# A decoder of two layers on one core: TensorE runs products that nobody reads ahead of the first steps of group 0 in three attentions

## The chip, the cores and the metric

One core of one Trainium2 chip runs the whole program. The metric is the device time of one execution in microseconds. The kernel before was timed in 3 runs, and one further execution was recorded by the profiler.

## The reference

The input x has 32 batches of 128 tokens of width 128, the context 32 x 128 x 96. Six blocks are added to x one after the other; each works on x normalised over its channels.

```python
x = x + self_attention(layernorm(x))              # layer 0, 16 heads of 8, rotary
x = x + cross_attention(layernorm(x), ctx)        # 16 heads of 8, scores clipped
x = x + gated_experts(layernorm(x))               # 8 experts, the best 2, and 2 shared
x = x + causal_attention(layernorm(x))            # layer 1, 16 heads of 8, rotary, causal
x = x + latent_attention(ctx, layernorm(x))       # 2 heads of 64, latents are the tokens of x
x = x + relu_experts(layernorm(x))                # 8 experts, the best 2, hidden size 512
```

An attention is softmax(q k^T / sqrt(d)) v, with projections for q, k, v and the output, and biases.

## The kernel before

The program is a row of phases, each a block in which the five engines have instruction streams of their own, with a barrier between. `load_setup` loads constants, x and weights. `attention` does self and cross attention in one phase and, in a later one, causal attention; `latent_attention` and `relu_experts` end the program. The 32 batches form 8 groups of 4 (`GB`), so that a group has 512 tokens (`GT`). Whatever concerns weights is done once a group, scores and softmax once a batch.

The order of the steps on each engine is written by hand in `ORDERS` (L195). For every batch n an engine goes through its list; a step such as `k^6` is done once a group, six batches ahead of the group's first batch, and a step without a number once a batch, ahead by what `AHEAD` says. In latent attention the number behind the name is always the lead. For self attention TensorE's list is

```python
"PE": "T s0 f0 m y f1 q^5 s1 k^6 x^7 w k2^6 q2^5 v^4",
```

so that group 0 begins with x, k, k2, q, q2 and v, one behind the other, before the first batch has any scores. The steps are these. `x` (L468) turns the normalised x into columns with 4 transposes into the bank PB; ScalarE rounds it (x_hi, L562) and VectorE makes the remainder (x_lo, L645). `k`, `k2`, `q`, `q2` (L482) project with three products of 512 columns into the same bank PB (L366 to L368), and each waits until VectorE (L613) or, in causal, ScalarE (L540) has read the projection before it. `v` projects with 12 products of 128 columns. POOL then adds the two halves of the rotation (L719), takes remainders (L728) and spreads keys and queries over the heads (L732). Per batch follow `s0` and `s1` (scores, L392, which VectorE reduces to maxima, L591), `m` (transpose of the maxima, L439), `T` (key scores, 12 products into the four banks T, L408 to L413), `f0` and `f1` (the maxima are subtracted, L425), the exponentials on ScalarE (L521), and `w` (weights times values, L452). In causal attention products with a constant (L377) start the scores with the mask.

Latent attention begins with `C` and `X` (L1658, transposes of context and x), then `P` (L1699, projection of a batch, five matrices in six products), `K` (L1709, transposes of q and k of a batch) and only then scores. TensorE starts once the setup and the mask rows (ScalarE, L1894) are there. `X` is followed on ScalarE by an affine step and a rounding, and on POOL by the remainder (L2178), for which `P` waits.

All of these products are fp32r except for the transposes and the weights times values. [...]

Of the kernel before, what the change touches and what calls it, by code (L numbers as in the profile page):

```python
# [19 lines left out]
P = 128  # L20
# [4 lines left out]
GT = GB * P  # L25
# [40 lines left out]
C_ID, C_ONES, C_MASK = 0, P, 5 * P  # L66
# [156 lines left out]
def attention(nc, phase, kinds, sb, bank, context=None, x_ready=None):  # L223
# [23 lines left out]
    cr = sb["const_r"]  # L247
# [13 lines left out]
    S, T = bank[:, 0:2 * GT], bank[:, 2 * GT:6 * GT]  # L261
# [13 lines left out]
    def steps(engine):  # L275


        for n in range(-10, NBT + 2):
            found = []
            for number, k in enumerate(kinds):  # L280
                order = ORDERS[k][engine].split()
                for place, step in enumerate(order):
                    name, _, lead = step.partition("^")
                    first = n + int(lead) if lead else n + AHEAD[name]
                    if first // B == number and not (lead and first % GB):
                        found.append((place / len(order), number, name, first // GB if lead else first))
            for _, _, name, i in sorted(found):
                yield name, i
# [9 lines left out]
    PIECES = ("k", "k2", "q", "q2", "v")  # L298
# [5 lines left out]
    with ExitStack() as ctx:  # L304
# [59 lines left out]
        def _(pe):  # L364
# [17 lines left out]
            def scores(n, pair):  # L382
                causal = kind(n) == "causal"
                if pair == 0:
                    pe.wait_ge(k_masked, n + 1)
                if 2 * n + pair > 0:
                    pe.wait_ge(max_done, 2 * n + pair)
                units = (2 * pair, 2 * pair + 1)
                if causal:
                    hide([S[:, u * GT:(u + 1) * GT] for u in range(2)], 0)  # L390
                for u in units:
                    mm = pe.matmul(s_bank(u), kq_hi[QUERY][(n // GB) % 2][rows_of(u), batch_cols(n)],  # L392
                                   k_hi_m[n % 2][rows_of(u), :, :], start=not causal, stop=True)
                mm.then_inc(scored, 1)

            def key_scores(n):
                causal, clip = kind(n) == "causal", kind(n) == "cross"
                pe.wait_ge(q_masked, 2 * n + 2)
                if n > 0:
                    pe.wait_ge(exp_done, 2 * n)  # L400
                g = (n // GB) % 2
                k_hi, k_lo, q_hi, q_lo = kq_hi[KEY][g], kq_lo[KEY][g], q_hi_m[n % 2], q_lo_m[n % 2]
                if causal:
                    for u in (0, 2):
                        hide([t_bank(u), t_bank(u + 1)], 1)
                out = [t_bank(u).rearrange("p (j q) -> p j q", j=U) for u in range(U)]
                for u in range(U):
                    pe.matmul(out[u], k_hi[rows_of(u), batch_cols(n)], q_hi[rows_of(u), :, :],  # L408
                              start=not causal, stop=False)
                for u in range(U):  # L410
                    pe.matmul(out[u], k_hi[rows_of(u), batch_cols(n)], q_lo[rows_of(u), :, :], start=False, stop=False)
                for u in range(U):
                    mm = pe.matmul(out[u], k_lo[rows_of(u), batch_cols(n)], q_hi[rows_of(u), :, :],  # L413
                                   start=False, stop=clip)
                    if clip and u % 2 == 1:
                        mm.then_inc(keyed, 1)

            def shift(n, pair):
                clip = kind(n) == "cross"
                if pair == 0:  # L420
                    pe.wait_ge(neg_max_done, n + 1)
                if clip:
                    pe.wait_ge(clipped, 2 * (n - B0) + pair + 1)
                for u in (2 * pair, 2 * pair + 1):
                    mm = pe.matmul(t_bank(u), cr[rows_of(u), C_ONES + u * P:C_ONES + (u + 1) * P],  # L425
                                   neg_max[n % 2][rows_of(u), :], start=False, stop=True, skip_group_check=clip)
                mm.then_inc(shifted, 1)

            def transpose_max(n):
                if kind(n) == "cross":  # L430
                    pe.wait_ge(max_clipped, n - B0 + 1)
                else:
                    pe.wait_ge(max_done, 2 * n + 2)
                if n > 0:
                    pe.wait_ge(neg_max_done, n)
                if n - 2 > 0:
                    pe.wait_ge(heads_done, n - 2)
                for j in range(U):
                    mm = pe.transpose(OM[:, j * P:(j + 1) * P], maxes[n % 2][:, j * P:(j + 1) * P], sb["ident"][:, :])  # L439
                mm.then_inc(max_transposed, 1)  # L440

            def weigh(n):
                pe.wait_ge(exp_done, 2 * n + 2)
                if n > 0:
                    pe.wait_ge(heads_done, n)
                pe.wait_ge(neg_max_done, min(n + 3, NBT))
                pe.wait_ge(pb_read, pb_uses["v", n // GB])
                for of, c in ((lambda u, j: V[(n // GB) % 2][:, n % GB, U * u + j, :], 0),
                              (lambda u, j: head_ones[:, j, :], P)):
                    for j in range(U):  # L450
                        for u in range(U):
                            mm = pe.matmul(OM[rows_of(u), c:c + P], of(u, j), probs[n % 2][:, u, j, :],  # L452
                                           start=j == 0, stop=j == U - 1)
                mm.then_inc(weighted, 1)
# [6 lines left out]
            def out_project(n):  # L461
                pe.wait_ge(heads_done, n + 1)
                bank_free("y", n)
                c = ATT[kind(n)] * P
                pe.matmul(PB[:, 0:P], o_t[n % 2][:, :], sb["w_out"][:, c:c + P], start=True, stop=True)\
                    .then_inc(out_projected, 1)
# [15 lines left out]
            def project(name, G):  # L482
# [9 lines left out]
                    mm = split_matmul(PB, w, (hi[:, :], lo[:, :]))  # L492
                mm.then_inc(projected, 1)

            for step, i in steps("PE"):
                if step == "T":
                    key_scores(i)
                elif step in ("f0", "f1"):
                    shift(i, int(step[1]))
                elif step == "y":  # L500
                    out_project(i)
                elif step in ("s0", "s1"):
                    scores(i, int(step[1]))
                elif step == "m":
                    transpose_max(i)
                elif step == "w":
                    weigh(i)
                elif step == "x":
                    transpose_x(i)
                elif step == "c":  # L510
                    transpose_c(i)
                else:
                    project(step, i)
# [950 lines left out]
def latent_attention(nc, phase, sb, ps, t, ready, routed):  # L1464
# [3 lines left out]
    X = sb["x"]  # L1468
    TR, PL, PC, KT, S, T, O, M = ps
    cr, cols = sb["const_r"], sb["cols"]  # L1470
    ident, ident_r = sb["ident"][:, :], cr[:, C_ID:C_ID + P]
# [21 lines left out]
    def steps(engine):  # L1493

        for n in range(-14, B + 24):
            for step in ORDERS["latent"][engine].split():
                name = step[:min(step.find(c) for c in "+-^" if c in step)]
                once = step[len(name)] == "^"  # L1500
                batch = n + int(step[len(name) + once:])
                if not 0 <= batch < B:
                    continue
                if not once:
                    yield name, batch
                elif name in ("L", "R", "R1", "EX", "GG", "PL"):
                    if batch in LAST:
                        yield name, LAST[batch]
                elif batch % GB == 0:
                    yield name, batch // GB  # L1510
# [12 lines left out]
    with ExitStack() as ctx:  # L1523
# [49 lines left out]
        at_or_after, start = buf("at_or_after", [P, N_TILES, E1]), buf("start", [P, N_TILES])  # L1573
# [78 lines left out]
        def _(pe):  # L1652
# [120 lines left out]
            pe.wait_ge(setup_steps, SETUP)  # L1773
            pe.wait_ge(masks_made, 1)
            pe.wait_ge(filled, FILLED)
            for step, i in steps("PE"):
                if step in ("X", "C"):
                    transpose_inputs(step, i)
                else:
                    {"P": project, "K": transpose_keys, "s": scores, "T": key_scores, "m": transpose_max, "f": shift,  # L1780
                     "w": weigh, "o": transpose_heads, "y": out_project, "Z": transpose_rows, "L": make_logits,
                     "R": count_earlier}[step](i)
# [641 lines left out]
```

## Time and profile before

| | us |
|---|---|
| median of 3 runs | 1434.62 |
| lowest and highest | 1428.91, 1439.69 |
| the profiled execution's own time | 1435.96 |
| its span in the profile | 1434.2 |
| TensorE, VectorE, ScalarE, POOL busy | 84%, 61%, 47%, 54% |
| phases: self and cross from | 20 |
| causal from | 700 |
| latent from | 967 |

The span is what the records of the execution cover, 1.8 us less than its own time. The profile names instructions by their line in the kernel, the tile written and the tile read; PE is TensorE, DVE VectorE, ACT ScalarE. Where a row gives idle time, the name behind it is what the engine waited for. [...]

### The profile page before, as it was taken

What the parts mean: (1) busy time and instruction counts of PE and PEld (TensorE: products, weight loads), DVE (VectorE), ACT (ScalarE), POOL (GpSimd) and SP (SyncE); (2) the same over time, 40 slices, a digit from 0 to 9 for tenths busy, and PEclk for the clock granted to TensorE, in tenths of its full rate; (3) what the DMA queues carried; (4) which work ended last, traced back from release to release, by engine and by line L of the source; (5) the groups of instructions that cost most, each with busy time, mean ns of one, the idle gap of its engine ahead of it and who ended that gap; (6) DMA issues with size and microseconds to landing.
All of it is one profiled execution on the core that took longest, in us unless ns stands there. A gap on an engine that the chain in (4) does not pass through costs nothing. (4 is left out here: it accounts for less than half of the span.)

```text
span 1434.2 us, 33962 instructions
## 1 busy us (share of the span) xinstructions
PE 1197.7 (84%) x12478; PEld 901.5 (63%) x12478; DVE 878.1 (61%) x2007; ACT 674.8 (47%) x1298; POOL 768.1 (54%) x870
## 2 busy tenths in 40 slices
PE   1899998788888874999799999984999993199992
PEld 0577775555555563666467777764899983088881
DVE  3688876599999955666255666555888843122223
ACT  1345444344545422455345545437888631055551
POOL 3777873555666511444455555525776757344452
PEclk9999998799999985999789999996999955599996
DMA  9910000000000000000000000000000001256656
GB/s 346 380 56 10 2 2 15 14 15 15 14 15 7 2 2 1 1 1 0 1 2 2 2 2 3 2 2 23 12 13 2 20 25 52 78 192 201 196 192 179
DMA packets 58863, 75.27 MB, mean 52 GB/s; under 512 B 13246, under 2 KB 40003, under 8 KB 58576
## 3 DMA queue, kind: packets, MB, share of 16 engines
q1 hardware_dynamic: 53328, 63.59, 13.8%
q0 software_dynamic: 4544, 8.47, 1.7%
q8 instruction: 101, 1.65, 0.5%
q10 hardware_dynamic: 832, 1.09, 0.2%
q14 instruction: 58, 0.48, 0.1%
HBM read 40.24 MB, written 31.70 MB: 50 GB/s over the span
## 5 line engine op out<-in xcount | busy, mean ns | idle before, releaser
L591 DVE TENSOR_REDUCE maxes<-bank 128x8 f32<-128x1024 f32 x192 | 234.4, 1221 | 56.6 <-PE bank L392 55.1
L521 ACT ACTIVATE self_probs<-bank 128x1024 f32<-128x1024 f32 x128 | 129.1, 1022 | 46.1 <-PE bank L425 45.7
L1429 POOL DMA_INDIRECT returned<-relu_y,relu_slots x78 | 76.7, 984 | 93.8 <-DVE relu_y L1404 81.3
L1372 ACT ACTIVATE relu_hidden<-bank,cols 128x256 f32<-128x256 f32 x156 | 74.0, 474 | 94.0 <-PE bank L1330 80.5
L528 ACT ACTIVATE self_neg_max<-bank 128x512 fp32r<-128x512 f32 x64 | 38.2, 597 | 149.9 <-PE bank L439 149.9
L732 POOL TENSOR_TENSOR self_k_hi_m<-self_kq_hi,const 128x512 fp32r<-128x512 f32 x64 | 66.6, 1041 | 78.4 <-ACT self_kq_hi L549 78.4
L1330 PE MATMUL bank<-relu_s,relu_w_tile 128*128 128x256 f32 x312 | 94.3, 385 | 0.5 <-DVE relu_s L1398 0.5
L1338 PE MATMUL bank<-relu_hidden,relu_w_tile 128*128 128x256 f32 x312 | 92.5, 379 | 0.0
L1398 DVE COPY relu_s<-bank 128x256 f32<-128x256 f32 x39 | 16.6, 425 | 110.5 <-issue 81.1
L597 DVE TENSOR_SCALAR bank<-bank 128x1024 f32<-128x1024 f32 x64 | 78.2, 1223 | 3.3 <-PE bank L413 3.3
L601 DVE RECIPROCAL self_recip<-bank 128x128 f32<-128x128 f32 x64 | 61.2, 957 | 30.2 <-PE bank L452 28.2
L2215 POOL DMA_INDIRECT routed<-latent_rows,latent_place_i x64 | 63.0, 984 | 30.8 <-issue 16.6
L732 POOL TENSOR_TENSOR causal_q_lo_m<-causal_kq_lo,const 128x512 fp32r<-128x512 f32 x32 | 33.3, 1041 | 84.5 <-PE bank L425 84.4
L452 PE MATMUL bank<-self_probs,values 128*32 128x128 f32 x2048 | 73.1, 286 | 1.4 <-ACT self_neg_max L528 1.2
L452 PE MATMUL bank<-self_probs,head_ones 128*32 128x128 f32 x2048 | 70.8, 280 | 0.0
L425 PE MATMUL bank<-self_neg_max,const_r 32*128 32x512 f32 x256 | 62.0, 475 | 9.7 <-DVE bank L597 6.3
L521 ACT ACTIVATE causal_probs<-bank 128x1024 f32<-128x1024 f32 x64 | 64.5, 1022 | 5.2 <-PE bank L425 2.7
L732 POOL TENSOR_TENSOR self_q_lo_m<-self_kq_lo,const 128x512 fp32r<-128x512 f32 x64 | 66.7, 1042 | 0.3 <-PE bank L425 0.2
L732 POOL TENSOR_TENSOR self_q_hi_m<-self_kq_hi,const 128x512 fp32r<-128x512 f32 x64 | 66.6, 1041 | 0.0
L452 PEld LDWEIGHTS bank<-self_probs,values 128*32 128x32 f32 x2048 | 54.9, 113 | 18.6 <-issue 15.9
L439 PE MATMUL bank<-ident,maxes 128*128 128x128 f32 x384 | 65.2, 294 | 0.5 <-POOL maxes L755 0.3
L1338 PEld LDWEIGHTS bank<-relu_hidden,relu_w_tile 128*128 128x128 f32 x312 | 59.3, 190 | 8.3 <-ACT relu_hidden L1372 0.2
(380 smaller groups left out, 3434.9 us busy)
## 6 DMA issues: line engine op xcount, KB each, us to landing
relu_w_tile<-in_w_ffn SPq DMA_DIRECT2D x39, 512.0 KB
routed<-blank SPq DMA_DIRECT2D x1, 19760.0 KB, 60.9
relu_slots<-routed SPq DMA_DIRECT2D x39, 130.0 KB
relu_back<-returned SPq DMA_DIRECT2D x16, 256.0 KB, 4.4
x_all<-in_x SPq DMA_DIRECT2D x8, 256.0 KB, 8.2
x_before<-x_all SPq DMA_DIRECT2D x8, 256.0 KB, 2.7
out_x<-x_all SPq DMA_DIRECT2D x8, 256.0 KB, 4.0
self_ctx_in<-in_ctx SPq DMA_DIRECT2D x8, 192.0 KB, 2.6
```

Of the source, the lines that this page charges most:

```text
L425: mm = pe.matmul(t_bank(u), cr[rows_of(u), C_ONES + u * P:C_ONES + (u + 1) * P], neg_max[n % 2][rows_of(u), :], start=False, stop=True, sk ...
L439: mm = pe.transpose(OM[:, j * P:(j + 1) * P], maxes[n % 2][:, j * P:(j + 1) * P], sb["ident"][:, :])
L452: mm = pe.matmul(OM[rows_of(u), c:c + P], of(u, j), probs[n % 2][:, u, j, :], start=j == 0, stop=j == U - 1)
L521: act.activation(probs[n % 2][:, 2 * pair:2 * pair + 2, :, :].rearrange("p u j q -> p (u j q)"), T[:, 2 * pair * GT:(2 * pair + 2) * GT], ...
L591: dve.tensor_reduce(out.rearrange("p j u -> p u j"), S.rearrange("p (u j k) -> p u j k", u=2, j=U), AX.X, ALU.max, negate=True).then_inc(m ...
L597: dve.tensor_scalar(t, t, CLAMP / scale, -CLAMP / scale, ALU.min, ALU.max).then_inc(clipped, 1)
L732: pool.tensor_tensor(out[n % 2][:, :, :], src[(n // GB) % 2][:, batch_cols(n)].bitcast(F32).unsqueeze(1).broadcast_to([P, U, P]), slots.un ...
L1330: pe.matmul(HT[i % 2][:, 0:TT], w_tile[t % NW][:, c * P:(c + 1) * P], s[t % 2][:, :], start=True, stop=True)\
L1338: pe.matmul(YT[t % 2][:, 0:TT], w_tile[t % NW][:, F1 + c * P:F1 + (c + 1) * P], hidden[i % C1][:, :], start=c == 0, stop=c == C1 - 1).then ...
L1372: act.activation(hidden[i % C1][:, :], HT[i % 2][:, 0:TT], ACT.Relu, bias=sb["cols"][:, bass.ds(r + (COL_RELU + c), 1)]).then_inc(hidden_d ...
L1429: pool.indirect_dma_start(returned[:, :], bass.IndirectOffsetOnAxis(ap=slots[t % NX][:, b, P:P + 1].bitcast(I32), axis=0), y[t % NY][:, b, ...
L2215: pool.indirect_dma_start(routed[:, :], bass.IndirectOffsetOnAxis(ap=place_i[u % 3][:, k, b:b + 1], axis=0), rows[G % 4][:, k, n % GB, :], ...
```

## The change

In both functions TensorE gets a helper `idle_passes` of 8 products of 512 columns. Their operands are constants (the identity and the block of ones), they write to T, which no step has in use yet, and nothing reads what they write. They wait for nothing. They are issued ahead of the steps x, k, k2, q, q2 and v of group 0 in self attention (6 times), x, k, q and v of group 0 in causal attention (4 times), and C, X of group 0 and P, K of batch 0 in latent attention (4 times). Cross attention's groups are numbered from 8 on, so that it has none. The helper stands in front of the step's own waits. Nothing is removed and no other engine's stream is changed.

```diff
@@ attention
+            def idle_passes():
+
+                for _ in range(8):
+                    pe.matmul(T[:, 0:GT], cr[:, C_ID:C_ID + P], cr[:, C_ONES:C_ONES + GT], start=True, stop=True)
+
             for step, i in steps("PE"):
+                if step in ("x",) + PIECES and i == 0:
+                    idle_passes()
@@ latent_attention
+            def idle_passes():
+
+                for _ in range(8):
+                    pe.matmul(T[:, :], ident_r, cr[:, C_ONES:C_ONES + GT], start=True, stop=True)
+
             for step, i in steps("PE"):
+                if step in ("X", "C", "P", "K") and i == 0:
+                    idle_passes()
```

`PIECES` is ("k", "k2", "q", "q2", "v").

TensorE's stream at the start of self attention, before (L472 is x, each trio L366 to L368 a projection):

```order
L363 UNCONDITIONAL_BRANCH
L472 MATMUL bank<-ident,self_xn 128x128 x4
L366 MATMUL bank<-self_x_hi,w_hi 128x512
L367 MATMUL bank<-self_x_lo,w_hi 128x512
L368 MATMUL bank<-self_x_hi,w_lo 128x512
L366 MATMUL bank<-self_x_hi,w_hi 128x512
L367 MATMUL bank<-self_x_lo,w_hi 128x512
L368 MATMUL bank<-self_x_hi,w_lo 128x512
L366 MATMUL bank<-self_x_hi,w_hi 128x512
```

and with the change, where L498 is the product of `idle_passes`:

```order
L363 UNCONDITIONAL_BRANCH
L498 MATMUL bank<-const_r 128x512 x8
L472 MATMUL bank<-ident,self_xn 128x128 x4
L498 MATMUL bank<-const_r 128x512 x8
L366 MATMUL bank<-self_x_hi,w_hi 128x512
L367 MATMUL bank<-self_x_lo,w_hi 128x512
L368 MATMUL bank<-self_x_hi,w_lo 128x512
L498 MATMUL bank<-const_r 128x512 x8
L366 MATMUL bank<-self_x_hi,w_hi 128x512
L367 MATMUL bank<-self_x_lo,w_hi 128x512
L368 MATMUL bank<-self_x_hi,w_lo 128x512
L498 MATMUL bank<-const_r 128x512 x8
```

Eight products have come ahead of the transposes and ahead of each projection; the order of the rest is the same. TensorE's stream at the start of latent attention, before (L1666 is C or X, L1654 to L1656 P):

```order
L1666 MATMUL bank<-ident,latent_cn 96x128 x4
L1666 MATMUL bank<-ident,latent_xn 128x128 x4
L1666 MATMUL bank<-ident,latent_cn 96x128 x4
L1654 MATMUL bank<-latent_w_hi,latent_x_hi 128x384
L1655 MATMUL bank<-latent_w_lo,latent_x_hi 128x384
L1656 MATMUL bank<-latent_w_hi,latent_x_lo 128x384
L1654 MATMUL bank<-latent_w_hi,latent_c_hi 128x256
L1655 MATMUL bank<-latent_w_lo,latent_c_hi 128x256
L1656 MATMUL bank<-latent_w_hi,latent_c_lo 128x256
```

and with the change, where the lines of this function are 7 numbers further on and L1786 is the product of `idle_passes`:

```order
L1786 MATMUL bank<-const_r 128x512 x8
L1673 MATMUL bank<-ident,latent_cn 96x128 x4
L1786 MATMUL bank<-const_r 128x512 x8
L1673 MATMUL bank<-ident,latent_xn 128x128 x4
L1673 MATMUL bank<-ident,latent_cn 96x128 x4
L1786 MATMUL bank<-const_r 128x512 x8
L1661 MATMUL bank<-latent_w_hi,latent_x_hi 128x384
L1662 MATMUL bank<-latent_w_lo,latent_x_hi 128x384
L1663 MATMUL bank<-latent_w_hi,latent_x_lo 128x384
L1661 MATMUL bank<-latent_w_hi,latent_c_hi 128x256
L1662 MATMUL bank<-latent_w_lo,latent_c_hi 128x256
```

The second group stands between C and X of group 0, the third between the C of group 1 and the first P; the fourth comes after three P, ahead of K.

## Rows read from the trace of the kernel before

**Rows 1.** The page: busy time of the engines (1), TensorE's clock in 40 slices (2).
```profile
PE 1197.7 (84%) x12478; PEld 901.5 (63%) x12478; DVE 878.1 (61%) x2007; ACT 674.8 (47%) x1298; POOL 768.1 (54%) x870
...
PEclk9999998799999985999789999996999955599996
```

**Rows 2.** Timeline of TensorE, self: start, us, instruction, count [idle before, releaser].
```profile
25.57 1.11 PE L472 MATMUL bank<-ident,self_xn 128*128 128x128 f32 x4 [25.57 <-ACT self_xn L556]
28.09 0.79 PE L366 MATMUL bank<-self_x_hi,w_hi 128*128 128x512 f32 x1 [1.41 <-DVE self_x_lo L645]
28.68 0.63 PE L367 MATMUL bank<-self_x_lo,w_hi 128*128 128x512 f32 x1
29.11 0.63 PE L368 MATMUL bank<-self_x_hi,w_lo 128*128 128x512 f32 x1
...
38.05 0.48 PE L366 MATMUL bank<-w_hi,self_x_hi 128*128 128x128 f32 x1 [0.84 <-DVE self_by_sin L613]
...
40.46 0.41 PE L368 MATMUL bank<-w_hi,self_x_lo 128*128 128x128 f32 x1
...
48.79 0.80 PE L366 MATMUL bank<-self_x_hi,w_hi 128*128 128x512 f32 x1 [0.84 <-DVE self_by_cos L613]
...
55.91 0.80 PE L408 MATMUL bank<-self_q_hi_m,self_kq_hi 32*128 32x512 f32 x4
...
57.36 0.48 PE L392 MATMUL bank<-self_k_hi_m,self_kq_hi 32*128 32x512 f32 x2
...
61.28 0.51 PE L408 MATMUL bank<-self_q_hi_m,self_kq_hi 32*128 32x512 f32 x4
```

**Rows 3.** Timeline of VectorE: the first instruction behind the barrier, self and causal.
```profile
20.25 0.87 DVE L637 BATCH_NORM_STATS2 self_stats<-x_all 128x6 f32<-128x128 f32 x4 [0.30 <-PEq L110]
...
700.45 0.87 DVE L637 BATCH_NORM_STATS2 causal_stats<-x_all 128x6 f32<-128x128 f32 x4 [0.32 <-PEq L889]
```

**Rows 4.** Windows around causal's start: from:to, length, busy of each engine, PEclk.
```profile
702.00:704.00 2.00, 0.00 (x0) 0.00 (x0) 0.00 (x0) 0.02 (x1) 1.68 (x4) 0.67 0.00 0
...
726.00:728.00 2.00, 1.74 (x9) 0.77 (x5) 1.11 (x1) 0.91 (x3) 1.00 (x1) 0.86 0.00 0
```

**Rows 5.** Timeline of TensorE, last product before causal and causal's start.
```profile
698.74 0.66 PE L1021 MATMUL bank<-ident,ffn_y 128*128 128x128 f32 x4 [0.69 <-ACT ffn_y L1051]
705.68 1.11 PE L472 MATMUL bank<-ident,causal_xn 128*128 128x128 f32 x4 [6.29 <-ACT causal_xn L556]
708.21 0.79 PE L366 MATMUL bank<-causal_x_hi,w_hi 128*128 128x512 f32 x1 [1.41 <-DVE causal_x_lo L645]
...
715.81 0.80 PE L377 MATMUL bank<-const_r 64*128 64x256 f32 x4
...
727.11 0.40 PE L367 MATMUL bank<-causal_x_lo,w_hi 128*128 128x512 f32 x1
727.35 0.39 PE L368 MATMUL bank<-causal_x_hi,w_lo 128*128 128x512 f32 x1
```

**Rows 6.** Timeline of TensorE and of ScalarE, latent's start.
```profile
978.64 1.09 PE L1666 MATMUL bank<-ident,latent_xn 128*128 128x128 f32 x4 [1.15 <-ACT latent_cf L1833]
984.68 1.09 PE L1666 MATMUL bank<-ident,latent_cn 128*96 128x128 f32 x4 [4.96 <-ACT latent_cn L1857]
985.55 0.69 PE L1654 MATMUL bank<-latent_w_hi,latent_x_hi 128*128 128x384 f32 x1
...
994.48 0.90 PE L1714 MATMUL bank<-ident,latent_unit 128*128 128x128 f32 x3 [2.27 <-DVE latent_unit L1947]
...
968.27 3.71 ACT L1894 ACTIVATE latent_mask_rows<-mask_by_row,latent_masked 128x4096 fp32r<-128x4096 uint8 x1 [7.25 <-POOL latent_one L2225]
```

**Rows 7.** A window of latent's start, in columns as in rows 4.
```profile
988.00:990.00 2.00, 1.82 (x8) 1.33 (x6) 0.77 (x6) 2.00 (x6) 1.14 (x4) 0.65 0.00 0
```

**Rows 8.** Timeline of POOL: a sum in self, the low part of x in latent.
```profile
38.07 1.28 POOL L719 TENSOR_TENSOR self_full<-self_by_cos,self_by_sin 128x512 f32<-128x512 f32 x1 [3.70 <-DVE self_by_sin L613]
...
984.23 1.27 POOL L2178 TENSOR_TENSOR latent_x_lo<-latent_xf,latent_x_hi 128x512 fp32r<-128x512 f32 x1
```

## Prediction

> **What bounds the kernel now.** I read the page first: TensorE is busy for 84% of the span and every other engine much less [rows 1]. The reader should see that an added TensorE instruction costs nothing only where the engine waits. The row PEclk says where TensorE's clock is high; it also shows the sag at the seventh and eighth slice, where self attention hands over to cross. Next come the three places of the change, in TensorE's order of time.
>
> Self attention, first steps [rows 2]. The record of the clock can't be trusted here: it says 0.9 or more from the start. But two products of 512 columns start 0.43 us apart (28.68 and 29.11), which is 1.2 GHz, and twelve of them take 1.45 us (55.91 to 57.36). The first four of the same twelve take 0.80 us there and 0.51 us at 61.28. So the clock rose near 57.4 us, after the engine had been almost without a gap since 48.79. Until then it ran at half speed for 32 us. In these 32 us the projections k, k2, q, q2 start 2.49 us apart, (38.05 - 28.09)/4. The engine idles 0.84 us in each of these steps but the first, waiting for VectorE to empty the one bank. VectorE's first instruction at 20.25 [rows 3] dates the barrier, so TensorE sits free from about 20.3 to 25.57.
>
> Causal attention [rows 4, 5]. The last product before it starts at 698.74 and ends near 699.4. The granted clock is at the 2.4 level until about 702.7 (0.67 as the mean of 702 to 704) and 1.2 GHz until about 726.5 (0.86 in 726 to 728). Here, at the high level, two products of 512 columns are 0.24 us apart (727.11, 727.35). Latent attention [rows 6, 7]: TensorE waits for the mask rows until 972.0 and begins C about 976.4 (X at 978.64, less 1.15 us idle and C's 1.1). It is at 1.2 GHz until about 989.4 (0.65 in 988 to 990), having been busy since 984.68.
>
> **The price of a group.** The change adds 14 groups of 8 products of 512 columns and removes nothing. A group is 8 x 0.43 = 3.4 us at 1.2 GHz and 8 x 0.24 = 1.9 us at 2.4 GHz. None of them waits for a semaphore, so each starts the moment the products before it are done. What is queued behind is the step itself, and after it everything in TensorE's order. Only idle time in front of a step hides a group.
>
> [...]
>
> **Self attention.** Group 1, before x, runs from 20.3 to 23.7 and is hidden. The four transposes begin at 25.57 as before and are off the array by 26.4. Group 2, before k, costs 3.4 us at 1.2 GHz and ends at 29.8, where k could start at 28.09: +1.7 us. From 25.57 on TensorE is never idle. When does the clock rise? Nearest rows: it rose 4.7 us after the engine became busy in latent (984.68 to 989.4) and 8.6 us after in self (48.79 to 57.4). Both ends are kept: 30.3 or 34.2 us. I take the earlier, since the gaps are gone altogether. A step is then 3 products and a group, 11 x 0.24 = 2.7 us, against 2.49 before. The release by VectorE needs 2.49 - 3 x (0.43 - 0.24) = 1.9 us and hides inside. With +0.4 for k's first product, v starts 1.7 + 0.4 + 4 x 0.2 = 2.9 us late. It has 12 products of 128 columns, which take 2.6 us at 1.2 GHz (38.05 to 40.46 and one more); it saves half, 1.3, so it ends 1.6 us late. For POOL's chain, which starts with the sum at 38.07 [rows 8], the delay is about 1.9 us. With the late rise all this is 2 us worse, since one step takes 11 x 0.43 = 4.7 us.
>
> From v to the key scores of batch 1 at 61.28 everything runs at 2.4 GHz instead of 1.2. It saves only where TensorE is the link: four projections of group 1 at 3 x 0.19 = 0.6 each (2.4), the twelve key score products, which go four at a time, 0.6, four pairs of scores at 0.3 (1.2), a transpose of maxima and the shifts 0.7, which go by the same ratio. That is 4.9 us; VectorE's reductions and POOL's masks, which lie between, do not get faster. Net 1.6 to 1.9 - 4.9 = -3 us, or -1 us with the late rise. I take -3. The bounds are -5 (no group lengthens anything) and +10.5 (the clock stays low through all groups: 1.7 + 4 x (4.7 - 2.49)).
>
> **Causal attention.** The barrier falls at about 700.3 [rows 3]. Group 1 then runs at 2.4 GHz to 702.2 and is hidden, since the transposes wait until 705.68. In before, the clock fell 3.3 us after the last product. Now 3.4 us of idleness (702.2 to 705.68) lie before the transposes, so it may or may not hold. If it falls, group 2 costs 3.4 us from 706.4 and k starts at 709.8 instead of 708.21: +1.6. The clock rises by 710.4, q and v follow 2.7 instead of 2.43 us apart (+0.5), and v saves 1.3: the first scores, 715.81 before, come 0.8 late. From there to 726.5 the scores with their mask products, k, q and a transpose save about 3 us on the chain; net -2.2. If the clock holds, group 2 ends at 708.3, nothing is late, and the net is -3.9. I take -2.8; the bounds are -3.9 and +6.1 (1.6 + 2 x 2.25, clock low throughout).
>
> **Latent attention.** Group 1 starts at 972.0 [rows 6] and ends at 975.4, hidden. Group 2, before X, sits between 977.2 and 980.6 at 1.2 GHz: X, at 978.64 before, comes 2 us late. Its consumer on POOL, the low part of x, stood behind other POOL work until 984.23 [rows 8], so this too is hidden. Then TensorE idles until 984.68, so it is at 1.2 GHz. Group 3 stands directly before P(0), which had no gap in front of it (985.55): +3.4 us, of which the higher clock gives back 0.6 in P(0) and P(1). ScalarE and the norms follow late; POOL's inverse had 1 us of slack, so K(0), at 994.48 before, is some 1.8 us late. Group 4 before it, 1.9 us, shares the 2.27 us gap that the profile shows there. Behind K(0) the clock is high instead of low, which gives back about 1 us (by the same halving of three more projections) before the engine is full again. Net +1; bounds -1 (all groups in gaps) and +4.5 (clock low: 3.4 + 1.1).
>
> **Sum.** -3 - 2.8 + 1 = -4.8 us. All three kinds of attention are followed by a long stretch in which TensorE is nearly full, so a shift at the start should carry to the end. Made against the profiled execution's own 1435.96 us it gives 1431.2; the median of the runs is 1.3 us lower, 1434.62, and would give 1429.8. I say 1430.5.
>
> [...]
>
> **The rivals.**
> 1. The groups lengthen the path by more than the clock returns. One mechanism, in self attention: the single bank PB passes between TensorE and VectorE, and each of k2, q, q2, v now has 3.4 us of passes in front of it where only 0.84 us was idle. Each step at 1.2 GHz costs 4.7 - 2.49 = 2.2 us. The gain of 4.9 is eaten when the delay at v exceeds it, that is when the clock rises later than about 37 us. For it: the record of the clock says nothing reliable there, and once it took 8.6 us. Against it: in latent and causal it rose sooner, with gaps between. If the clock never rose within the groups: +10.5 + 6.1 + 4.5 = +21, 1457 us. With the rise a step or two late in each place: +2 to +6, about 1439.
> 2. The clock rises within or right after group 1 and holds over the short gaps: -5 - 3.9 - 1 = -10, about 1425. For it: group 1 is 3.4 us without a gap. Against it: in before the clock fell 3.3 us after the last product ahead of causal, and in latent 3.4 us of idleness remain ahead of 984.68.
> 3. The start gets shorter but POOL or VectorE, not TensorE, sets when batch 1 begins, or the clock's sag at the handover to cross (slices 7 and 8) falls otherwise and takes the gain or doubles it: about 0, 1435.
>
> **How the numbers follow.** Forecast (-2 to -8): 0.50. Rival 1: 0.15, of which 0.02 for the full 21 us. Rival 2: 0.15. Rival 3: 0.20. The forecast's own terms reach from 1427 to 1434; the runs of before spread over 11 us by themselves. The range takes in rival 2, rival 3 and the mild part of rival 1, and a median's own spread beyond them: 1421 to 1441. This measurement tells a difference from no change at about 1%, 14 us; faster by more would need every bound at its best and luck besides (0.04), slower by more needs the clock to stay low (0.03), and the rest, 0.93, lies within 1%.
>
> **What would show it.** In the changed profile: the 8 passes before x lie ahead of 25.6 us; spacing drops from 0.43 to 0.24 us between 29 and 34 us; v's first product starts near 41 us; the key scores of batch 1 start near 58 instead of 61.3; in causal the first scores start near 716.6 less the shift, and in latent P(0) is about 3 us further behind its C(1) than now. I am wrong if products are still 0.43 us apart after v, if v starts later than 43 us, or if the key scores of batch 1 start no earlier than before.

## The result, and the profile after

The changed kernel took 1440.03 us in the median of 20 runs (1434.59 to 1448.00), the kernel before 1435.95 us in 20 runs (1428.91 to 1445.33). The ratio is 1.0034, with a 95% interval from 1.0020 to 1.0048: slower by 0.34%, 4.9 us. I had forecast 1430.5 us, 4 to 5 us faster.

The profiled execution of the changed kernel took 1448.00 us, the longest of the 20. So the two traces are 12 us apart where the medians are 4 us apart, and the traces can't simply be subtracted. The page of the changed kernel, in the form of [rows 1]:

```profile
PE 1233.3 (85%) x12590; PEld 929.0 (64%) x12590; DVE 876.0 (61%) x2007; ACT 674.0 (47%) x1298; POOL 767.0 (53%) x870
...
PEclk9699998899999985899969999997999975599996
```

TensorE is 36 us busier. In the row PEclk three slices are lower than before: the second (36 to 72 us, 6 instead of 9), the 17th (578 to 615 us, in the experts, 8 instead of 9), and the 21st (723 to 759 us), where 6 stands and before had 7 and 8 in the 20th and 21st. The second and the 21st lie right behind the steps that the change touches.

PEclk is the granted clock of TensorE as a share of full speed. Low means 0.50 from here on and high 1.00. In the changed kernel's trace products of 512 columns start 0.427 us apart at 0.50 (26.07 to 29.06 us) and 0.227 us apart at 1.00 (35.22 to 38.88). These are the levels that the prediction calls 1.2 and 2.4 GHz.

TensorE's timeline at the start of self attention, in the columns of [rows 2]; L498 is the product of the added groups:

```profile
19.78 3.38 PE L498 MATMUL bank<-const_r 128*128 128x512 f32 x8 [19.78 <-PEq L110]
25.10 0.65 PE L472 MATMUL bank<-ident,self_xn 128*128 128x128 f32 x4 [1.93 <-ACT self_xn L563]
25.51 3.33 PE L498 MATMUL bank<-const_r 128*128 128x512 f32 x8
...
29.70 2.00 PE L498 MATMUL bank<-const_r 128*128 128x512 f32 x8
...
39.10 0.22 PE L366 MATMUL bank<-w_hi,self_x_hi 128*128 128x128 f32 x1
...
41.62 0.63 PE L472 MATMUL bank<-ident,self_xn 128*128 128x128 f32 x4 [1.07 <-DVE values L630]
43.12 0.79 PE L392 MATMUL bank<-self_k_hi_m,self_kq_hi 32*128 32x512 f32 x2 [0.87 <-POOL self_k_hi_m L739]
45.23 0.79 PE L392 MATMUL bank<-self_k_hi_m,self_kq_hi 32*128 32x512 f32 x2 [1.33 <-DVE maxes L598]
...
55.57 0.80 PE L408 MATMUL bank<-self_q_hi_m,self_kq_hi 32*128 32x512 f32 x4
...
62.94 0.80 PE L408 MATMUL bank<-self_q_hi_m,self_kq_hi 32*128 32x512 f32 x4
```

Up to v nearly all came as forecast. Group 1 is hidden, group 2 takes 3.3 us, the next ones 2.0 us, and v's first product starts at 39.10. What follows is the surprise: the four transposes at 41.62 still take 0.63 us, but the scores at 43.12 take 0.79, and at 55.57 and 62.94 the first of the twelve key score products take 0.80 us. That is the size at the low clock of [rows 2]. The key scores of batch 1 start at 62.94 instead of 61.28. The clock itself, in windows of this stretch (from:to, length, busy time of PE, PEld, DVE, ACT, POOL, then PEclk, DMA share and GB/s):

```profile
26.00:28.00 2.00, 2.00 (x6) 1.55 (x6) 1.47 (x5) 0.38 (x1) 0.40 (x1) 0.50 1.06 382
28.00:30.00 2.00, 2.00 (x7) 1.55 (x7) 0.48 (x5) 0.00 (x0) 1.21 (x3) 0.64 1.06 383
...
42.00:44.00 2.00, 1.04 (x5) 0.29 (x3) 0.74 (x2) 0.60 (x1) 2.00 (x3) 0.77 1.06 383
44.00:46.00 2.00, 0.77 (x3) 0.33 (x3) 1.96 (x5) 0.00 (x0) 2.00 (x3) 0.50 1.05 381
...
68.00:70.00 2.00, 2.00 (x32) 1.57 (x34) 1.56 (x2) 1.83 (x4) 1.37 (x2) 0.50 1.06 381
70.00:72.00 2.00, 2.00 (x56) 1.70 (x50) 0.55 (x2) 0.23 (x1) 2.00 (x3) 0.90 1.06 380
```

It rose at 29.4 us, near the 30.3 forecast. It had been high once before, toward the end of group 1: that group took 3.38 us and the transposes behind it 0.65, where e1 below, low throughout, shows 3.75 and 1.12. Behind the idle 1.93 us ahead of the transposes it fell at 26.0, so that group 2 ran at the low clock (0.50 in 26 to 28). It fell again at 43.1, behind v, where the engine works only 1.04 of 2 us, and then stayed at 0.50 until 70.4, 27 us, through windows in which TensorE was full or nearly so. In before it was high from 57.4 to 241.9. Causal attention has the same, in the columns of [rows 5] and [rows 4]:

```profile
715.10 0.77 PE L472 MATMUL bank<-ident,causal_xn 128*128 128x128 f32 x4 [3.15 <-ACT causal_xn L563]
715.52 3.65 PE L498 MATMUL bank<-const_r 128*128 128x512 f32 x8
719.02 0.39 PE L366 MATMUL bank<-causal_x_hi,w_hi 128*128 128x512 f32 x1
...
725.48 0.50 PE L377 MATMUL bank<-const_r 64*128 64x256 f32 x4
...
727.74 0.50 PE L377 MATMUL bank<-const_r 64*128 64x256 f32 x4 [1.33 <-DVE maxes L598]
...
730.09 0.80 PE L377 MATMUL bank<-const_r 64*128 64x256 f32 x4 [0.83 <-DVE maxes L598]
...
752.82 0.60 PE L425 MATMUL bank<-causal_neg_max,const_r 32*128 32x512 f32 x2
```

```profile
728.00:730.00 2.00, 1.25 (x10) 0.64 (x8) 1.29 (x2) 0.60 (x1) 2.00 (x3) 0.79 0.00 0
730.00:732.00 2.00, 1.92 (x7) 1.28 (x8) 0.96 (x2) 0.00 (x0) 2.00 (x3) 0.50 0.00 0
...
750.00:752.00 2.00, 2.00 (x17) 1.08 (x14) 0.36 (x1) 0.00 (x0) 0.00 (x0) 0.50 0.00 0
752.00:754.00 2.00, 2.00 (x12) 1.29 (x13) 0.00 (x0) 1.08 (x2) 0.00 (x0) 0.74 0.00 0
```

The first scores (725.48) come 14.6 us behind the phase's first VectorE aggregate, at 710.89; before it was 14.35 (715.81 and 701.46). So the groups cost the path 0.2 us here, although the clock fell at 715.5, behind 3.15 us of idleness, and group 2 took 3.65 us; it was back at 718.9. But the clock falls again at 729.2, in the gaps of 1.33 and 0.83 us around the scores, and is back only at 753.1. Those are 24 us at the low clock, and TensorE is busy in all but the first microsecond of them. In before the clock fell as well and was low for just as long, from 702.7 to 726.6; but the first 13 us of that were idle time and sparse projections.

Latent attention, in the columns of [rows 6]; L1786 is the added product:

```profile
999.95 1.09 PE L1673 MATMUL bank<-ident,latent_cn 128*96 128x128 f32 x4 [5.21 <-ACT latent_cn L1871]
1000.69 3.76 PE L1786 MATMUL bank<-const_r 128*128 128x512 f32 x8
1004.25 0.52 PE L1661 MATMUL bank<-latent_w_hi,latent_x_hi 128*128 128x384 f32 x1
...
1011.06 2.67 PE L1786 MATMUL bank<-const_r 128*128 128x512 f32 x8
1013.56 0.49 PE L1721 MATMUL bank<-ident,latent_unit 128*128 128x128 f32 x3
```

Here a group took 3.8 us in front of P(0) at the low clock (998.8 to 1005.6), where 3.4 was forecast, and 2.7 us in front of K(0), where 1.9 was.

To see what was the change and what was chance I cut all traces into stages. Each entry is the distance between the starts of two VectorE instructions: phase start of self (time 0) to the first output of self (o_t of batch 0), and so on. The causal stage runs from its first aggregate of moments to the third o_t, the latent stage from its first aggregate to the fifth heads, all in us:

| kernel | self, start | self to cross, o_t 30 to 40 | experts, groups 0 to 3 | causal, start | latent, start |
|---|---|---|---|---|---|
| before | 67.83 | 87.59 | 36.36 | 55.57 | 58.57 |
| the change | 72.48 | 86.86 | 43.03 | 61.54 | 61.20 |
| the change, again (e8) | 64.09 | 87.80 | 36.34 | 61.53 | 59.89 |
| self groups (e1) | 65.86 | 90.12 | 36.44 | 55.60 | 58.64 |
| causal groups (e2) | 67.87 | 87.79 | 42.85 | 57.14 | 57.72 |
| causal groups, again (e7) | 68.08 | 91.60 | 36.38 | 61.54 | 58.62 |
| latent groups (e3) | 67.98 | 88.96 | 43.08 | 55.55 | 59.44 |
| hidden groups (e4) | 66.35 | 91.54 | 36.37 | 55.40 | 58.41 |
| causal bridged (e5) | 68.05 | 87.78 | 36.34 | 54.79 | 59.58 |
| all bridged (e6) | 64.08 | 91.22 | 43.03 | 53.32 | 58.98 |
| self and causal bridged (e9) | 62.14 | 87.97 | 36.40 | 53.30 | 58.25 |
| self bridged (e10) | 63.83 | 91.18 | 36.30 | 55.56 | 58.73 |
| bridges alone (e11) | 67.96 | 88.02 | 36.39 | 54.77 | 59.61 |

The columns of the handover to cross and of the experts jump by 4 and 6.7 us between kernels that are equal there. The 6.7 us of the experts are in the first trace of the changed kernel and in e2, e3 and e6; in each of them the clock came back only at 585 to 589 us instead of 564 to 575. They have nothing to do with the change: in e3 nothing is changed ahead of the experts, and the change's second trace (e8) does not have them. The rest of the program, behind the fifth heads of latent, is no steadier: it took 405.4 us in before, 399.5 and 407.1 in the two traces of the change, and 397.8 to 412.2 in all. So the time of a single trace says little here. The stretch behind causal's start is steady: from the third o_t to the first aggregate of the latent phase all 13 traces take 213.1 us. What causal's start loses or wins is there in full at the end of that phase.

### The profile page after: what moved, and what is told of

It reads as the page before. It is cut to its first block and busy times, and to the rows that moved or that the text cites. A ratio compares the mean times of both kernels' runs of the same rounds, so it can differ in the third digit from the quotient of the medians.

```text
span 1446.2 us, 34185 instructions
## 1 busy us (share of the span) xinstructions
PE 1233.3 (85%) x12590; PEld 929.0 (64%) x12590; DVE 876.0 (61%) x2007; ACT 674.0 (47%) x1298; POOL 767.0 (53%) x870
## 5 line engine op out<-in xcount | busy, mean ns | idle before, releaser
L1249 POOL TENSOR_TENSOR ffn_hidden<-ffn_product,ffn_gate 128x512 f32<-128x512 f32 x32 | 40.9, 1281 | 46.9 <-ACT ffn_gate L1058 40.0
## 6 DMA issues: line engine op xcount, KB each, us to landing
routed<-blank SPq DMA_DIRECT2D x1, 19760.0 KB, 61.5
```

## The experiments

In all of them the ratio is that of 5 rounds against the kernel before on the same chip, with its 95% interval. Absolute times of different batches are not compared, since the kernel before itself took 1437.35, 1443.36 and 1434.75 us in the three batches.

**The parts one by one.** Self alone (e1):

```diff
-                if step in ("x",) + PIECES and i == 0:
+                if kinds[0] == "self" and step in ("x",) + PIECES and i == 0:
                     idle_passes()
@@ latent_attention
-                if step in ("X", "C", "P", "K") and i == 0:
-                    idle_passes()
```

> Only the 6 groups of self attention. Theory F (the clock is won too early: it rises near 30 us, falls again near 43 us in the gaps behind v, and comes back only near 70 us instead of 57): +2 to +5 us against before, low clock in most of 44 to 65 us, key scores of batch 1 (61.28 us before) at 62 or later. Rival O (only the groups' own time on TensorE costs, the clock is neutral): k, k2, q, q2 are 2.5 us apart as before, v ends no later, so 0 to +1 us. Rival N (the loss is luck in stretches that the change does not touch): 0.

Measured: 1.0002 (0.9976 to 1.0028). The trace is 2.0 us ahead at the first output; the clock rose near 29 us (group 2 still took 3.4 us, k's first product behind it 0.39), fell at 46.1 and was back at 52.9. So the low spell can be as short as 6.8 us. With the two traces of the change there are now three draws of this stage, that is three outcomes between which chance decides: 72.48, 64.09 and 65.86, mean 67.5, against 67.8 to 68.1 in the six traces that have no groups in self (before, e2, e3, e5, e7 and e11). Three traces that spread over 8 us fix no mean, but the runs of e1 agree with it: no difference, within 4 us. The expectation of theory F, +2 to +5 us and the key scores of batch 1 at 62 or later, was wrong for self; they started at 59.30.

Causal alone (e2), the same with `kinds[0] == "causal"`:

> Only the 4 groups of causal attention. Theory F: the clock falls within some 5 us behind v and stays low for over 15 us while TensorE is full: the second output of causal attention +3 to +6 us later, counted from the phase's first instruction. Rival O: at most +1 us. Rival N: 0.

Measured: 1.0066 (1.0042 to 1.0089), on 6 runs only. The trace has a low spell from 727.1 to 740.7, 14 us of full work, and the stage is 1.6 us longer. The interval excludes O and N; but the trace shows less than the ratio, so it was run again (e7):

> The causal groups alone once more, for the interval and a second trace. Theory F: again +3 to +10 us, with the clock down for 10 to 24 us behind v. If it comes out within 2 us of before, the first result was chance.

Measured: 1.0050 (1.0025 to 1.0075) on 12 runs, 7 us. The windows of its trace:

```profile
722.00:724.00 2.00, 1.52 (x10) 0.90 (x10) 0.97 (x2) 0.06 (x1) 2.00 (x3) 0.95 0.00 0
724.00:726.00 2.00, 1.27 (x6) 0.82 (x6) 1.26 (x2) 0.54 (x1) 2.00 (x3) 0.50 0.00 0
...
744.00:746.00 2.00, 2.00 (x20) 1.45 (x18) 1.01 (x1) 0.00 (x0) 0.00 (x0) 0.50 0.00 0
746.00:748.00 2.00, 2.00 (x16) 1.01 (x8) 0.00 (x0) 0.43 (x1) 0.00 (x0) 0.57 0.00 0
748.00:750.00 2.00, 2.00 (x44) 1.50 (x46) 1.03 (x1) 1.93 (x3) 0.75 (x1) 1.00 0.00 0
```

The clock fell at 723.8 and rose at 747.7, again 24 us, and the stage is 6.0 us longer than in before. Most of what is left to the changed kernel is this.

Latent alone (e3), with the first condition taken out and the second left in:

> Only the 4 groups of latent attention. Here the groups before P and K stand on the path: Rival O gives +2 to +3 us in this phase, Theory F adds nothing to that (in the trace with the change the clock was high from 1012 us on). Rival N: 0.

Measured: 1.0011 (0.9993 to 1.0029). The stage is 0.9 us longer than in before, and 1.3 and 2.6 in the two traces of the change. The ratio can't tell +1.6 us from nothing. Nor do the traces settle it: the eight without groups in latent reach from 57.72 to 59.61 (mean 58.7), the four with all of them from 58.98 to 61.20 (mean 59.9). About +1.2 us is likely, not shown.

Only the groups in idle time (e4):

```diff
-                if step in ("x",) + PIECES and i == 0:
+                if step == "x" and i == 0:
                     idle_passes()
-                if step in ("X", "C", "P", "K") and i == 0:
+                if step == "C" and i == 0:
                     idle_passes()
```

> Only the three groups that stand in idle time (before x in self and causal, before C in latent). Rival O: 0, since nothing on the path gets longer. Theory F: 0 as well, within 1 us, since the clock has no reason to be higher behind v than before; the first projections may start at the high level. If it is 2 us or more slower, the groups do harm by what they do to the clock later, not by their place.

Measured: 0.9988 (0.9964 to 1.0012), no difference. The causal stage is 55.40 us, as in before, and the first output of self is 1.5 us ahead. In causal the clock fell at 712.0 and was back at 732.4.

**The change once more** (e8, no edit):

> [...] Theory F: +3 to +6 us against before; in causal a fall of the clock within 6 us behind v. The places before causal (between cross attention and the experts) may come out anywhere within 8 us of the first trace.

Measured: 1.0045 (1.0020 to 1.0070). In causal the clock falls at 716.6 and rises at 740.5, 24 us again, and the stage is 61.53 us to the first trace's 61.54. In self it is 3.7 us faster than before: there it was high from behind group 1 on (the transposes at 25.29 take 0.66 us, group 2 2.11), fell at 44.2, and came back at 51.0. So the first trace's loss in self was a draw, the loss in causal was not.

**Bridging the gaps behind v.** If the falls are what cost, products in those gaps should turn the loss into a gain. In causal (e5):

```diff
-            def idle_passes():
+            def idle_passes(count=8):
 
-                for _ in range(8):
+                for _ in range(count):
...
+            BRIDGE = {("s1", 0): 6, ("x", 1): 2, ("s0", 1): 4}
...
+                if kinds[0] == "causal" and (step, i) in BRIDGE:
+                    idle_passes(BRIDGE[step, i])
```

with the groups of causal attention kept and those of self and latent left out.

> The 4 groups of causal attention and, in the gaps behind v, 6 products before the second scores of batch 0, 2 before x of group 1 and 4 before the first scores of batch 1. Theory F: the clock does not fall behind v, and the loss turns into a gain: 4 to 8 us faster than the run with the causal groups alone, against before -3 to +1 us; the second output of causal 2 to 4 us earlier within the phase than before. Rival O: another 0 to 2 us slower than the causal groups alone, since TensorE has more to do. If the clock falls all the same, the gaps are not what sends it down.

Measured: 1.0016 (0.9995 to 1.0037), against 1.0050 for e7 in the same batch. By the ratios that is 5 us less, and the stage went from 61.54 to 54.79 us, 0.8 below before. The windows:

```profile
718.00:720.00 2.00, 2.00 (x12) 1.17 (x10) 0.94 (x1) 0.00 (x0) 1.92 (x3) 1.00 0.00 0
...
730.00:732.00 2.00, 2.00 (x17) 1.41 (x16) 1.09 (x4) 1.97 (x3) 1.46 (x3) 1.00 0.00 0
...
734.00:736.00 2.00, 2.00 (x20) 1.36 (x18) 0.88 (x1) 0.15 (x1) 2.00 (x3) 0.50 0.00 0
...
738.00:740.00 2.00, 2.00 (x48) 1.49 (x50) 1.22 (x1) 1.97 (x4) 0.94 (x1) 1.00 0.03 8
```

The clock is high from 710.1 to 734.0, through all the gaps; then it falls once, for 3.4 us. Rival O wanted a slower kernel than e7, since TensorE has 12 more products; it is out. Against before the whole is still not faster.

In all (e6), with the whole change kept:

```diff
+            BRIDGE = {"causal": {("s1", 0): 6, ("x", 1): 2, ("s0", 1): 4},
+                      "self": {("x", 1): 5, ("s0", 0): 4, ("s1", 0): 6, ("k2", 1): 4}}[kinds[0]]
```

> The whole change and such bridges in causal and in self (5 products before x of group 1, 4 and 6 before the first and second scores of batch 0, 4 before k2 of group 1). Theory F: self gains 3 to 5 us at the key scores of batch 1, causal 2 to 4, latent loses 2: -2 to -6 us against before. Rival O: slower than the change itself.

Measured: 0.9948 (0.9923 to 0.9973), 7.5 us faster than before (expected 2 to 6), where the change in the same batch was 0.45% slower. Its timeline at the place of the first surprise:

```profile
41.12 1.35 PE L498 MATMUL bank<-const_r 128*128 128x512 f32 x5
42.34 0.63 PE L472 MATMUL bank<-ident,self_xn 128*128 128x128 f32 x4
42.74 1.17 PE L498 MATMUL bank<-const_r 128*128 128x512 f32 x4
43.87 0.50 PE L392 MATMUL bank<-self_k_hi_m,self_kq_hi 32*128 32x512 f32 x2
44.30 1.67 PE L498 MATMUL bank<-const_r 128*128 128x512 f32 x6
...
52.90 0.51 PE L408 MATMUL bank<-self_q_hi_m,self_kq_hi 32*128 32x512 f32 x4
53.23 0.40 PE L411 MATMUL bank<-self_q_lo_m,self_kq_hi 32*128 32x512 f32 x4
```

The products of scores take 0.50 us where they took 0.79, and the first key scores start at 52.90 instead of 55.57 in the change and 55.91 in before, although 19 more products stand ahead of them. Here the clock stays high until 237 us.

Without the latent groups (e9: e6 without the last condition):

> Self and causal groups with their bridges, none in latent. Theory F with the latent groups as a plain cost of 1 to 2.5 us on the path: 1 to 3 us faster than the version that has them too, -6 to -10 us against before. If it is slower than that version, the latent groups are worth having.

Measured: 0.9961 (0.9938 to 0.9984). The expected 1 to 3 us against e6 are not there; the intervals overlap almost wholly. Its latent stage is 0.7 us shorter. Whether the latent groups cost anything in the end stays open.

Self bridged, nothing else (e10; shown against e6, and the condition in latent attention is out as well):

```diff
-                if step in ("x",) + PIECES and i == 0:
+                if kinds[0] == "self" and step in ("x",) + PIECES and i == 0:
                     idle_passes()
-                if (step, i) in BRIDGE:
+                if kinds[0] == "self" and (step, i) in BRIDGE:
```

> Self groups and the self bridges, nothing else. Theory F: the clock rises near 30 us and never falls before 230 us; the first output of self near 64.1 us instead of 67.8 in the trace, -3 to -5 us against before. Rival O: 0 to +1.

Measured: 0.9941 (0.9918 to 0.9964), 8.5 us faster than before (expected 3 to 5), with 63.83 us to the first output where before has 67.83. The stage explains 4 us and the ratio says 5 to 12; the rest lies in later stages of one trace and can't be pinned down from it. Rival O is out here too. With causal groups and bridges on top (e9) the ratio is no better, 0.9961, although the causal stage is 2.3 us shorter. Whether the bridges of self would do without its groups was not run.

The causal bridges without groups (e11; shown against e6, latent's condition out again):

```diff
-                if step in ("x",) + PIECES and i == 0:
-                    idle_passes()
-                if (step, i) in BRIDGE:
+                if kinds[0] == "causal" and (step, i) in BRIDGE:
                     idle_passes(BRIDGE[step, i])
```

> The three bridges in causal without the four groups. Theory F says that the clock must be up before the gaps come: it has fallen ahead of the phase as in before and comes back only some 20 to 24 us after that fall, so the bridges run at 1.2 GHz and cost their own time where they exceed the gaps: third output of causal 55 to 57 us into the phase, 0 to +2 us in all. If it is 2 us or more faster, the early groups are not needed.

Measured: 1.0018 (0.9990 to 1.0046), so nothing that can be told. The stage is 54.77 us, 0.8 below before. The three bridges in its timeline:

```profile
720.89 2.77 PE L498 MATMUL bank<-const_r 128*128 128x512 f32 x6
...
724.45 0.73 PE L498 MATMUL bank<-const_r 128*128 128x512 f32 x2
...
725.38 1.18 PE L498 MATMUL bank<-const_r 128*128 128x512 f32 x4
```

The clock fell at 706.3, 1.2 us behind the first aggregate as in before, and was back at 723.3, after 17.1 us and not the expected 20 to 24. So only the first bridge ran at the low clock (2.77 us for 6 products), the other two at the high one (1.18 us for 4). The stage is as short as with the groups (54.79 in e5), a little below the 55 to 57 expected. In causal the bridges alone did what groups and bridges did in e5; only e6 and e9, at 53.3, were shorter. Whether the first bridge brought the clock back sooner one trace can't show.

## Why the prediction was wrong

**The step that failed** is the second half of the self estimate and its twin in causal: "From v to the key scores of batch 1 at 61.28 everything runs at 2.4 GHz instead of 1.2", and "From there to 726.5 the scores ... save about 3 us on the chain". Both took the clock, once up, for up. I had asked only when it rises and never what would send it down again behind v, though the fall at the start of causal was in my own rows. The runs show that it falls 2.7 to 5.2 us behind v, in gaps of no more than 1.33 us each, at all seven places that have groups before v and no bridges (three in self, four in causal). It then stays low for 7 to 27 us, and that time is nearly full of work: TensorE is busy for 88 to 92% of it in self and 96 to 97% in causal. The last of my own signs of being wrong came true with it: the key scores of batch 1 started at 62.94, later than before.

**Point by point.** Price of a group: 3.3 to 3.8 us at the low clock and 2.0 us at the high one, against 3.4 and 1.9. No run shows the frequencies of 1.2 and 2.4 GHz by which the forecast names the two levels; what they show is PEclk at 0.50 and 1.00, with products of 512 columns 0.427 and 0.227 us apart. Self up to v: v's first product at 39.10, forecast 41; the rise at 29.4, forecast 30.3 or 34.2. I had v late by 2.9 us and it was 1.1; part of that is luck, since in this trace the clock had been high for a moment under the transposes and the start of group 2, and in e1, where it had not, v was 1.6 us late. The gain behind it is real where the clock holds: e6, e10 and e9 reach the first output 3.8, 4.0 and 5.7 us sooner than before, where I had 3. Without bridges the stage came out at +4.6, -3.7 and -2.0, on average nothing, where I had -3. Causal: the first scores late by 0.2 us, forecast 0.8 or nothing; the stage +6.0, +6.0, +6.0 and +1.6 us, mean +4.9, where I had -2.8. With bridges it is -2.3 (e6, e9) and -0.8 (e5, where the clock fell once at 734.0), so the possible gain was of the right size as well. Latent: +1 to +2.6 against before, forecast +1. Counted from the group ahead of P(0) (in before from P(0) itself), K(0) came 3.9, 2.4 and 2.1 us later in the change, e8 and e3, where I had 1.8; in the first of them the clock fell once more, at 1009.1, ahead of the fourth group.

**The sum** by measured stages is -0.3 + 4.9 + 1.6 = +6 us, to a measured +4.9 (2.9 to 6.9) and, in e8, +6.5. Only its causal term stands clear of the scatter; the other two are means of three traces each. The ratios of the three parts add to +0.02, +0.5 or +0.66, and +0.11%, that is 0.6 to 0.8%, a little more than the change's own 0.34 and 0.45%, but within their intervals.

**The rivals.** Rival 1 had the right sign and the wrong mechanism. It had the passes keep PB's projections waiting while the clock stays low; the clock rose by 29.4 us in every trace with self's groups and within 3.4 us of its first fall in causal, and v was never late by more than 1.8 us (in self 39.83 in e6 against 38.05, in causal 13.2 us behind the first aggregate in the change against 11.6). The first half of rival 2 happened: in both traces of the change the clock rose within or right behind group 1, and in e8 it held over the gap to the transposes. That it holds behind v as well is what the bridges bring about (to 236 or 237 us in e6, e9 and e10). Rival 3 named luck at the handover to cross; it is there (86.9 to 91.6 us), and larger luck sits at the start of the experts, but neither goes with the change.

**Why causal loses and self does not.** In before the clock is low for a while in each of the three phases: in self until 57.4, in causal from 702.7 to 726.6, in latent from 968.9 to 989.4. The low time of causal begins 1.2 us behind the start of the phase's first aggregate, and more than half is spent on idling and on projections with waits between them, so that it costs little. With the groups it falls 4.3 to 4.7 us behind the first aggregate for 3.4 us, is high up to v, and falls again 18.0 to 18.3 us behind the aggregate in all four traces, where the scores of the first batches follow with hardly a gap. So the long low time comes 17 us later than in before. In the three traces with the spell of 24 us the stage is 6 us longer, with 14 us it is 1.6. In self TensorE runs nothing before the phase. In before its products start at the low spacing (0.427 us, 28.68 and 29.11), and the clock rises only at 57.4; the groups win back about 29 to 43 us and lose what the draw of the second spell takes, 7 us in two traces and 27 in one. That the groups move the fall from idle into busy time is shown by the traces with and without them and by the bridges; why a spell lasts 7, 14 or 24 us with the engine full stays open.

With self's groups the clock did not rise at the same product in all traces: in one trace of the changed kernel toward the end of group 1 (22.6), to be lost at 26.0 and come back at 29.4; in the other right behind group 1 (23.7), to stay until 44.2; with self's groups alone (e1) at 29.0, in the seventh product of group 2. The first stage of the two traces of the changed kernel took 72.48 and 64.09 us.

## What to carry to other kernels

Before you spend products to raise TensorE's clock, look at what the engine does right behind them (the falls here came 2.7 to 5.2 us behind v): if gaps follow, bridge these too or leave it. In causal here the long low time came 17 us later than in before, into busy time, and the stage took 61.5 us instead of 55.6. In this kernel the groups with bridges in self attention are worth 0.6%, and the change, with groups in all three attentions and no bridges, costs 0.3%. And where single executions of one kernel differ by 15 us, compare traces by stages and repeat the trace, or a draw is taken for the cause.

## What the runs showed of the hardware

- At causal's start the clock stayed at 0.50 for 23.9 us in seven of the 13 traces (702.7 to 726.6 in before, 729.2 to 753.1 in the change), whether TensorE was idle at first or full nearly all through. In the other six the longest spell there was 3.4 to 20.4 us. In the experts of the change it stayed low from 569.5 to 589.2 although TensorE was busy for 19.67 of these 19.7 us, most of that time on products of 512 columns.
- At the start of self the record of the clock is no measurement: in before it says 1.00 (28 to 30, 54 to 56) while products of 512 columns start 0.427 us apart, until 57.4 us, and in e1 it does so until 29.0. There the spacing was the measure, 0.427 us at the low clock and 0.227 at the high one.
- 12 products of 128 columns take 2.6 us at the low clock (38.05 to 40.67 in before) and 1.3 us at the high one (39.10 to 40.39 in the change): 0.21 and 0.11 us each, so a quarter of the columns for half of the 0.427 and 0.227 us of a product of 512.
